# Attention stage: row maxima moved SBUF to SBUF from SyncE's queue, expert weights rounded by GpSimd, second pair's queries and keys loaded from GpSimd's queue

## The reference, cut to what matters

```python
qkv = x @ Wqkv + bqkv                                   # 16 heads of 32
scores = einsum('bhid,bhjd->bhij', q, k) * scale + alibi_causal_bias
attn = softmax(scores, axis=-1)
out = einsum('bhij,bhjd->bhid', attn, v) ...@ Wo + bo
```

## Time and profile before

| | |
|---|---|
| median of 3 runs | 1769.5 us (1769.17 to 1769.53) |
| profiled execution, its own time | 1764.4 us |
| its span | 1762.7 us |
| busy over the span | PE 89%, PEld 62%, DVE 56%, ACT 34%, POOL 37% |
| granted clock of PE, mean | 0.945 of full |
| attention stage | 167.7 to 804.4 us |

### The profile page before, as it was taken

One profiled execution on the slowest core, in us unless ns is written; L12 is line 12 of the kernel. 1 busy time (PEld: TensorE's weight loads), 2 busy tenths in 40 slices (PEclk: granted clock), 3 DMA queues, 4 the chain that ended last, 5 costly groups with the idle time before them and its releaser, 6 DMA issues. The chain is left out here.

```text
span 1762.7 us, 22247 instructions
## 1 busy us (share of the span) xinstructions
PE 1567.7 (89%) x7890; PEld 1088.6 (62%) x7890; DVE 988.6 (56%) x1698; ACT 603.4 (34%) x1138; POOL 648.5 (37%) x530
## 2 busy tenths in 40 slices
PE   5998888899999999997979999489999964799997
PEld 4886544454545545444767777367777753688886
DVE  7664766777888778833535545355565361132332
ACT  3211245555555555562212212354232320122221
POOL 4000034276887688682256666252021010000000
PEclk9998789999999999998989999789999986899999
DMA  6876513644536445134621121342022015420210
GB/s 228 269 231 186 116 23 82 124 101 90 152 103 139 111 132 119 49 102 166 228 91 60 54 73 49 111 149 73 30 91 96 1 49 185 155 96 1 95 48 24
DMA packets 99029, 188.51 MB, mean 107 GB/s; under 512 B 28890, under 2 KB 37994, under 8 KB 97050
## 3 DMA queue, kind: packets, MB, share of 16 engines
q1 hardware_dynamic: 77044, 120.60, 24.4%
q0 software_dynamic: 13648, 51.61, 9.9%
q10 hardware_dynamic: 8234, 14.94, 2.4%
HBM read 121.97 MB, written 65.16 MB: 106 GB/s over the span
## 5 line engine op out<-in xcount | busy, mean ns | idle before, releaser
L999 ACT ACTIVATE att_probs<-att_ring 128x512 f32<-128x512 f32 (+3 forms) x640 | 298.4, 537 | 287.6 <-DVE att_ring L1036 148.4
L1027 DVE TENSOR_REDUCE att_maxes<-att_ring 128x2 f32<-128x1024 f32 (+7 forms) x366 | 339.0, 947 | 83.8 <-PE att_ring L921 75.0
L956 PE MATMUL att_outp<-att_probs,att_vs 128*64 128x512 f32 (+3 forms) x1280 | 277.4, 556 | 0.3 <-ACT att_att L982 0.3
L1592 PE MATMUL glu_u<-glu_xh,glu_w 128*128 128x512 f32 x352 | 139.5, 396 | 19.9 <-DMA glu_xl<-zn_lo 19.9
L956 PEld LDWEIGHTS att_outp<-att_probs,att_vs 128*64 128x64 f32 x1280 | 79.7, 139 | 122.8 <-issue 72.7
L1593 PE MATMUL glu_u<-glu_xl,glu_w 128*128 128x512 f32 x352 | 139.2, 395 | 0.0
L1651 DVE TENSOR_TENSOR glu_hid<-glu_sig,glu_u 128x512 f32<-128x512 f32 x44 | 30.3, 688 | 170.4 <-ACT glu_sig L1631 170.4
L1665 POOL DMA_DIRECT2D out<-glu_y x4 | 3.1, 787 | 314.5 <-DVE glu_y L1656 253.8
L921 PE MATMUL att_ring<-route_wbh,route_wah 100*128 100x512 f32 (+2 forms) x320 | 104.7, 411 | 14.3 <-PEq L57 6.4
L942 PE MATMUL att_ring<-route_wah,route_wbh 102*128 102x512 f32 (+2 forms) x320 | 106.5, 410 | 10.2 <-ACT att_probs L999 5.5
L921 PE MATMUL att_ring<-moew_wbl,moew_wal 100*128 100x512 f32 (+2 forms) x320 | 99.7, 385 | 15.8 <-ACT att_probs L999 12.1
(11 more groups left out here) (274 smaller groups left out, 3374.2 us busy)
## 6 DMA issues: line engine op xcount, KB each, us to landing
att_q_raw<-in_w POOLq DMA_DIRECT2D x48, 352.0 KB, 4.0
w_ternary<-att_q_out POOLq DMA_DIRECT2D x24, 352.0 KB, 2.6
glu_w<-w_ternary ACTq DMA_DIRECT2D x9, 768.0 KB, 11.9
xn<-qkv_x SPq DMA_DIRECT2D x4, 1024.0 KB, 7.2
q_hi<-qkv_hi SPq DMA_DIRECT2D x16, 256.0 KB, 4.1
q_lo<-qkv_lo SPq DMA_DIRECT2D x16, 256.0 KB, 4.5
k_hi<-qkv_hi SPq DMA_DIRECT2D x16, 256.0 KB, 2.9
k_lo<-qkv_lo SPq DMA_DIRECT2D x16, 256.0 KB, 3.5
```

The lines of the kernel that those rows point to most:

```text
L956: last = pe.matmul(outp[v_cols(h), off:CH], vs[p % 2][:, kt, v_cols(h)], probs[:, g % 4, h, off:CH], start=kt == 0, stop=kt == TT * (c + 1 ...
L999: act.activation(probs[:, g % 4, h, off:CH], ring[:, rg.banks["score", g][h], off:CH], ACT.Exp).then_inc(exped, 1)
L1027: last = dve.tensor_reduce(maxes[:, hs, t, g:g + 1], banks[:, :, 0:width], AX.X, ALU.max)
L1592: pe.matmul(u[:, n % 2, :], w[:, k, s], xh[par][:, k, :], start=k == 0, stop=False)
```

## The change

Three edits, all in the attention stage.

1. `store_rows` and `fetch_rows` go, with the tensor in HBM. `move_rows` copies the maxima from `rows` straight into the operand's two extra rows by eight small DMAs per chunk (for each head and each of the four partition blocks: 2 partitions, 4 runs of 128 bytes). SP issues them all, except four of chunk 0, which ACT issues (its second head). ACT issues no DMA after that. PE waits for all eight.
2. `WeightSplit.hi_by` does the rounding on POOL as a copy to the rounded type, right ahead of the subtraction. ACT's 16 roundings go.
3. Pair 1's queries and keys (12 DMAs) go from SP's queue to POOL's, with a semaphore of their own (`second_in`), ahead of POOL's first weight pieces. They still wait for chunk 1's maxima. Pair 1's values go to SP's step g = 16.

```diff
+    def hi_by(self, pool, j):
+        src, hi, lo = self.pieces[j]
+        pool.wait_ge(self.loaded[j % self.depth], 16 * (j // self.depth + 1))
+        pool.tensor_copy(hi, self.stage[j % self.depth][:, 0:src.shape[-1]]).then_inc(self.hi_done, 1)
...
-        def store_rows(eng, n):
-            eng.wait_ge(rows_ready, n + 1)
-            for r in range(2 * 2):
-                eng.dma_start(rows_d[n, r, :].rearrange("(t b q) -> b t q", t=TT, q=HD), rows[n % 2][r:P:HD, :, :]
-                              ).then_inc(rows_stored[n % 2], 16)
-
-        def fetch_rows(eng, n):
+        def move_rows(eng, n, heads=(0, 1)):
+            p, c = divmod(n, NCH)
+            eng.wait_ge(rows_ready, n + 1)
+            for h in heads:
+                to = qs[p % 2][SROWS:SROWS + 2, h, c * CH:(c + 1) * CH].bitcast(F32).rearrange("a (t b q) -> a t b q", t=TT, q=HD)
+                for b in range(P // HD):
+                    eng.dma_start(to[:, :, b, :], rows[n % 2][b * HD + h:b * HD + h + 3:2, :, :]).then_inc(row_in[n % 2], 16)
...
-            store_rows(sp, 1)
-            fetch_rows(sp, 1)
-            sp.wait_ge(row_in[1], 16)
-            queries(1, first)
-            queries(1, late)
-            keys(1, whole)
-            load_values(sp, 1)
+            move_rows(sp, 0, (0,))
+            move_rows(sp, 1)
...
+                if g == SECOND_VALUES_AT:
+                    load_values(sp, 1, v_in[1])
...
-            store_rows(act, 0)
-            fetch_rows(act, 0)
+            move_rows(act, 0, (1,))
...
-                for n in range(NN):
-                    if fetched_at(n) == g:
-                        fetch_rows(act, n)
-                piece, between = divmod(g - SPLIT_FROM, SPLIT_EVERY)
-                if g >= SPLIT_FROM and not between and piece < len(ahead):
-                    ws.hi(act, piece)
...
-            pool.wait_ge(exped, 1)
+            pool.wait_ge(row_in[1], ROW_MOVES)
+            queries(pool, 1, first, second_in)
+            queries(pool, 1, late, second_in)
+            keys(pool, 1, whole, second_in)
             for j in range(ws.depth):
                 ws.load(pool, j)
             router.store(pool)
             for j in range(len(ahead)):
+                ws.hi_by(pool, j)
                 ws.lo(pool, j)
```

More of the change, by code:

```diff
@@ L811, in attention_stage @@
         pair_in = [st.sem(f"pair_in{i}") for i in range(2)]
-        v_in, row_in, rows_stored = ([st.sem(f"{n}{i}") for i in range(2)] for n in ("v_in", "row_in", "rows_stored"))
+        v_in, row_in = ([st.sem(f"{n}{i}") for i in range(2)] for n in ("v_in", "row_in"))
+        second_in = st.sem("second_in")
         unit_made, unit_masked, unit_taken = st.sem("unit_made"), st.sem("unit_masked"), st.sem("unit_taken")
@@ L840, in stored_at, with moved_at @@
-        def stored_at(n):
+            for h in heads:
+                to = qs[p % 2][SROWS:SROWS + 2, h, c * CH:(c + 1) * CH].bitcast(F32).rearrange("a (t b q) -> a t b q", t=TT, q=HD)
+                for b in range(P // HD):
+                    eng.dma_start(to[:, :, b, :], rows[n % 2][b * HD + h:b * HD + h + 3:2, :, :]).then_inc(row_in[n % 2], 16)
+        def moved_at(n):
             made = step_of_unit(min(last_unit_of(n) + (MAX_LAG if last_unit_of(n) >= FIRST_LEAD else 0), NG - 1))
-            return made + STORE_LAG if made >= 0 else -1
@@ L845, in fetched_at, with load_values @@
-        def fetched_at(n):
-            return min(stored_at(n) + FETCH_LAG, first_step_of(n) - FETCH_BEFORE) if stored_at(n) >= 0 else -1
+            return made + MOVE_LAG if made >= 0 else -1
         def masks_before(g):
             return sum(on_diagonal(i) for i in range(g))
-        def load_values(eng, p):
+        def load_values(eng, p, arrived):
             eng.dma_start(vs[p % 2][:, :, HD:3 * HD], v_d[:, p * 2 * HD:(p + 1) * 2 * HD].rearrange(
-                "(t p) d -> p t d", p=P)).then_inc(v_in[p % 2], 16)
+                "(t p) d -> p t d", p=P)).then_inc(arrived, 16)
@@ L855, in _, with queries, keys @@
+        def queries(eng, p, t, arrived):
+            load_queries(eng, qs[p % 2], p, t, qh_d, ql_d, aq_d, arrived)
+        def keys(eng, p, t, arrived):
+            load_keys(eng, ks[p % 2], p, t, kh_d, kl_d, ak_d, arrived)
+        first, late, whole = slice(0, T - CH), slice(T - CH, T), slice(0, T)
         @block.sync
         def _(sp):
[L857 to L861, removed]
@@ L863, in _ @@
-            first, late, whole = slice(0, T - CH), slice(T - CH, T), slice(0, T)
             def store(p, c):
@@ L915, in unit_product @@
                 if p and v % NS == 0:
-                    pe.wait_ge(pair_in[par], (p + 1) // 2 * 3 * LOADS * 16)
+                    if p == 1:
+                        pe.wait_ge(second_in, 3 * LOADS * 16)
+                    else:
+                        pe.wait_ge(pair_in[par], p // 2 * 3 * LOADS * 16)
                 out = [ring[:, b, :] for b in rg.banks["unit", v]]
```

33 lines of the change are left out of this document (14 added, 19 removed).

## The result

The kernel after takes 1752.8 us (median of four runs, 1747.4 to 1774.8) against 1769.5 before (four runs, 1769.2 to 1770.5). The ratio is 0.9894, with a 95% interval of 0.987 to 0.9919: 14 to 23 us faster. The forecast was 1747.5, with a range of 1739.5 to 1758. The profiled execution took 1754.25 us (span 1752.3), 10 us less than the one before.

The account below looks back on a forecast made before the run. PE bounds attention's steady part; early holes come from ACT or SP blocked on unneeded work. Terms 7.6 + 3.0 + 8.4 + 2.0 + 1.0 = 22.0 us give 1742.4 profiled, 1747.5 median, range 1739.5 to 1758.

Parts of the forecast that it names:

- Pair 1's loads off SP: Start of attention: moving these loads to POOL frees SP's full queue and closes A; 7.6 us, ends 4.1 and 9.5.
- the maxima by moves: Eight moves per chunk replace stores and ACT's fetches, so C goes: 2.4 us, up to 3.5, taken as 3.0.
- ACT thinner: ACT's list without roundings and fetches: part of PE's other 14 waits for ACT (4 us) goes, taken as 1.0 us.
- A: Hole about 210 to 225 us: chunk 2's maxima stored late behind pair 1's loads on SP; DVE idles 7.6 us.
- C: Hole at 257.56 us: PE waits 2.41 us for chunk 3's maxima, whose fetch ACT issued late.
- Rounding on POOL: Takes ACT out of D and E: 8.4 us from D, 2.0 net from E.
- D: Hole at 281.49 us: PE waits 6.43 us for ACT, which waits for a weight piece to round; 8.4 with low clock.
- E: Hole at 320.27 us: PE waits 4.04 us, ACT on a weight piece; 5.4 us, less 3.4 returning as pair 2's wait.
- POOL's bill: POOL's cost of rounding: CASTs 0.95 and 0.5 us, sixteen pieces in 56 us, ending near 752, before PE.
- no wait over 2 us for ACT: Sign in PE's trace: no wait this long for ACT between 205 and 330 us.
- about 425 matmuls at a clock above 0.95: Sign in PE's window from 200 to 300 us, instead of 308 matmuls before.
- PE's end at 782: Sign: PE's last attention matmul near 782 us, where it ended at 803.7 before.

Follow-up runs that it names:

- corners without the scatter: Router's indirect DMAs replaced by POOL clears: before 1754.0 us, before plus rounding on POOL 1752.1, before plus moves and loads 1745.3, after 1747.2.
- a_hi_act: Kernel after with the rounding back on ACT and off POOL: 1755.1 us (5 runs), ratio 0.9939 to before.
- a_scatter_late: Kernel after with the router's scatter moved behind POOL's sixteen weight pieces: 1763.0 us (10 runs), ratio 0.9996 to before.

## Why the prediction was right, and where it was off

**Pair 1's loads off SP (7.6 us) and the maxima by moves (3.0).** Right in mechanism and nearly in size. The 13 us issue is gone, the moves are in time, POOL's loads are in without a wait. The corners without the scatter measure 8.7 us for both, where the sum had 10.6, and part of "ACT thinner" on top. Putting only the loads back brings A back as 5.22 us of waiting for the moves, in the one profile that there is of it. C was not worth its 3.0: PE's wait for chunk 3's maxima is 0.62 us with rounding on POOL alone and is absent in the second profile of before. Eight moves take 5.30 us to issue, 0.66 each and not the 0.55 forecast from the stores; it costs nothing, as SP has the time.

**Rounding on POOL (8.4 + 2.0).** This is the mis-sized term: the step that took D for a constant cost of ACT's rounding. The part alone gives 1764.0 against 1766.7 with a ratio that includes 1, and 1.9 or nothing without the scatter. D was in one profile of before and not in the other, and not in `a_hi_act`, where ACT rounds too; it goes with a fetch of the list that came 13.24 us behind the last scatter instead of 6.4 to 7.4. Some 8 us of the sum rested on one wait of one execution, while the loss that the other profiles with the dense scatter have, DVE's stop, was not in that profile at all. E did what was forecast: 4.04 us turned into 2.32 for pair 2's keys, of which I had 3.4 (0.5 to 4.3 in the other profiles with rounding on POOL).

**DVE's rows.** The prediction took DVE's rows for reductions and additions on PSUM. The small copies and subtractions behind each maximum and the router's places are between SBUF tiles, and `a_scatter_late` shows them held up by POOL (2.14 us instead of 0.20). The trace of before had it already: the copy behind a maximum (L1049) takes 0.48 us in the mean of 32, and 0.17 at its fastest.

**POOL's bill.** CAST 1.04 and 0.62 us (forecast 0.95 and 0.5); pieces from 263.3 to 324.2, 61 us (forecast 56, done near 320); last store 754.3 (752), 38 us ahead of PE. It never bounds.

**The signs.** Right were the SP issue, no idling of ACT put down to a DMA, the first unit of pair 1, the CASTs, POOL's end and no wait of PE for a move. Wrong were "no wait over 2 us for ACT" (8.31), "about 425 matmuls at a clock above 0.95" (353 at 0.93) and PE's end at 782 (792.3). Even without any stop the window has only 385 to 392, so 425 was too many: I had let the steady rate begin at 200, while pair 1's start (3.3 us) and pair 2's loads (3.5) remain, and PE at the start goes at DVE's pace (from 205 to 330 it waits 5.1 us for DVE's maxima).

**Ten us of PE's end.** 2.6 of them are a later start of the stage in this one execution (170.38 against 167.75). The stage itself got 14.1 us shorter where the sum had 22, 7.9 short. The stop cost more than that: 8.31 us, 1.95 ahead of it, and 1.5 for eight matmuls at the low clock (3.45 against 1.94), together 11.8. So between these two profiles the terms gave some 4 us more than I had; 1.1 of it is E, the rest isn't told apart.

**What is shown of the stop, and what is not.** Eight profiles have the dense scatter and seven of them the stop (the longest idle of DVE in each is 4.55 to 7.94 us); six have no dense scatter and none has it. The stop moved with the scatter, went when it was spread, and went with direct stores. It was in the kernel before as well, so the change neither made nor cured it. The one dense profile without it, the first of before, is also the one where the list was fetched late. Not shown is what holds DVE: its data is ready and the profile names no releaser that fits. What POOL's computing did to DVE above looks otherwise: there instructions were drawn out and ended with POOL's, while here none starts, and the masks and maxima that stand still work on PSUM with at most a constant from SBUF. That it is another mechanism is argued and not shown.

**How much of it was luck.** That the time fell 5 us from the forecast is in part luck. D, 8.4 us of the sum, was not in the second profile of before, and DVE's stop, which the sum didn't have, took more than that from the kernel after. The 17 us come from four runs of each kernel; before had 1766.7, 1768.5 and 1765.7 in the later sets where it had 1769.5 there, and ten further runs of after have a median of 1765.7, which is outside the range that was forecast. The run of 1774.8 may be of the same kind as the seven slower ones of those ten, which reach 1775.6.

**What stays open.** The 17 us were not found again on a further chip, where 7 of 10 runs of the kernel after were as slow as before. The slower profile differs in its waits for pairs' loads (11.8 us against 4.6). Its clock at the start is lower too (0.59 against 0.71 from 170 to 200), but that of the kernel with direct stores is 0.61, and it is the fastest. What decides between the groups wasn't tried. With the scatter spread all four runs were under 1749 us, which four runs can't settle.

## What to carry to other kernels

Before a hole of some us is put into a sum, look whether a second execution has it; two profiles of one kernel differed here by a hole of 6 us in the one and two stops of 8 us together in the other, 30 us apart. A transfer issued ahead of time is only free if nothing urgent is queued behind it: moving twelve loads to an idle queue was the best part of this change. Indirect DMAs beside a busy DVE are worth trying spread among other work instead of in a row: here that was 5 to 20 us.

## What the runs showed of the hardware

- Beside sixteen indirect DMAs of 128 values, one each 1.27 us, DVE stood idle for 4.55 to 7.94 us at a time, most of it with its data ready, in seven of eight profiles. At 3.2 to 9.4 us apart they did not do it, nor did sixteen direct stores 0.53 us apart. Spreading them was worth 20.5 us of 1765.7 on one chip by the medians, and some 5 against the faster runs of the dense kernel; part of the 20.5 is in later waits for loads, 5.7 us in the spread kernel and 11.8 in the other.
- A small operation of DVE between SBUF tiles took 2.14 and 2.38 us instead of 0.20 and 0.23 beside a subtraction of POOL, and ended with it. The Trainium skill (page "SBUF — State Buffer", Who interferes with whom) has a lock for this: a tensor_scalar in a two-port mode, and a DVE instruction with two SBUF inputs beside a GpSimd one that reads SBUF, wait for the whole of the other, while a tensor_reduce never does. The trace agrees: the tensor_scalars end with POOL's subtractions, DVE's subtraction of two SBUF tiles (1.08 us instead of 0.18) with POOL's CAST, and a reduction at 220.46 beside a subtraction of POOL takes its 0.18 us. In which mode the tensor_scalars ran no row tells. The page's warning that the prediction weighed, a DVE copy that keeps GpSimd from writing descriptors, is the same lock the other way, and no run shows it.
- A move of 1 KB between SBUF tiles takes 0.66 us of SP's queue, and eight of them had landed within 1.28 us of the last issue; the short runs of 128 bytes did no harm that a run shows.
